# Order of mask tests, cell totals and scatter runs in a graph network kernel

## The reference

```python
edge_index = jnp.stack([src, dst])
h = jnp.maximum(_layernorm(x, axis=-1), 0.0)
x = x + _L0_gnn_ref(h, edge_index, ...)   # messages relu(bn([h[src], edge_rep[dst]] @ W1)), summed over dst, then over src
h = jnp.maximum(_layernorm(x, axis=-1), 0.0)
x = x + _L1_gnn_ref(h, edge_index, edge_weight, ...)   # three rounds of: sum over edges of norm * out[row]
...                                        # layer 2: attention over the first 3125 edges; layer 3: gated sum over edges
```

## Time and profile before

| what | us |
|---|---|
| median of 3 runs | 3788.69 (3786.29 to 3794.76) |
| the profiled execution | 3754.2 |
| its span | 3752.5 |
| TensorE busy | 2420.2 |
| VectorE busy | 2253.4 |
| ScalarE busy | 1348.1 |
| GpSimd busy | 1744.7 |

### The profile page before, as it was taken

One profiled execution on the slowest core, in us unless ns is written; L12 is line 12 of the kernel. 1 busy time (PEld: TensorE's weight loads), 2 busy tenths in 40 slices (PEclk: granted clock), 3 DMA queues, 4 the chain that ended last, 5 costly groups with the idle time before them and its releaser, 6 DMA issues. The chain is left out here.

```text
span 3752.5 us, 38369 instructions
## 1 busy us (share of the span) xinstructions
PE 2420.2 (64%) x11894; PEld 1975.0 (53%) x11894; DVE 2253.4 (60%) x4208; ACT 1348.1 (36%) x2765; POOL 1744.7 (46%) x1293
## 2 busy tenths in 40 slices
PE   5787544444444357750004998607999999973998
PEld 4422244444444345540004884406889888962688
DVE  6899677777777788860003442403564564535788
ACT  4488444434444200000002333303434434433676
POOL 0258877667667676767776767770000000024000
PEclk8888755555555568885557999758999999975999
DMA  9992355656556766651115661116546545512255
GB/s 350 355 322 26 49 169 170 169 168 173 167 164 172 161 158 184 187 124 0 0 0 122 177 156 1 1 0 171 171 132 187 173 132 171 162 53 53 84 174 177
DMA packets 339434, 521.99 MB, mean 139 GB/s; under 512 B 144970, under 2 KB 226691, under 8 KB 332195
## 3 DMA queue, kind: packets, MB, share of 16 engines
q1 hardware_dynamic: 197144, 446.27, 36.8%
q0 software_dynamic: 135920, 61.61, 14.2%
q10 hardware_dynamic: 6170, 11.66, 1.0%
HBM read 370.82 MB, written 148.58 MB: 138 GB/s over the span
## 5 line engine op out<-in xcount | busy, mean ns | idle before, releaser
L1054 PE MATMUL banks<-rows_r,lhs_r 128*128 128x448 f32 x3500 | 897.9, 371 | 517.4 <-issue 358.3
L1054 PEld LDWEIGHTS banks<-rows_r,lhs_r 128*128 128x128 f32 x3500 | 664.7, 190 | 588.6 <-issue 507.5
L669 POOL DMA_INDIRECT counts<-wts x391 | 615.2, 1573 | 378.2 <-issue 202.7
L678 POOL DMA_INDIRECT weights<-wts x391 | 634.0, 1621 | 253.5 <-issue 247.6
L498 DVE SCALAR_TENSOR_TENSOR ring_r<-ring,dinv,rows_r 128x896 fp32r<-128x896 f32 (+1 forms) x300 | 303.3, 1033 | 440.7 <-ACT rows_r L486 440.6
L686 POOL DMA_INDIRECT reg<-tab_p,w x440 | 426.1, 968 | 230.2 <-issue 120.5
L1054 PE MATMUL banks<-ring_r,lhs_r 128*128 128x448 f32 x1750 | 525.1, 370 | 0.0
L486 ACT ACTIVATE rows_r<-ring,dinv 128x896 fp32r<-128x896 f32 (+1 forms) x300 | 284.9, 951 | 515.0 <-PE banks L1054 345.1
L496 DVE TENSOR_TENSOR ring_r<-ring,rows_r 128x896 fp32r<-128x896 f32 x200 | 191.9, 973 | 445.1 <-ACT rows_r L484 444.8
L732 POOL DMA_INDIRECT el<-tab_l,base_i x25 | 24.0, 959 | 810.3 <-DMA tab_l<-reg 803.0
L484 ACT ACTIVATE rows_r<-ring 128x896 fp32r<-128x896 f32 x200 | 170.6, 857 | 510.2 <-DMA ring<-counts 358.9
(11 more groups left out here) (250 smaller groups left out, 3842.2 us busy)
## 6 DMA issues: line engine op xcount, KB each, us to landing
ring<-weights SPq DMA_DIRECT2D x225, 448.0 KB, 3.3
ring<-counts SPq DMA_DIRECT2D x150, 448.0 KB, 3.3
zbuf<-reg SPq DMA_DIRECT2D x220, 256.0 KB, 3.0
reg<-zbuf SPq DMA_DIRECT2D x55, 1024.0 KB, 4.7
counts<-ring SPq DMA_DIRECT2D x25, 1568.0 KB, 15.8
weights<-ring SPq DMA_DIRECT2D x25, 1568.0 KB, 17.6
ring<-cells SPq DMA_DIRECT2D x38, 448.0 KB, 4.3
ring<-weights SPq DMA_DIRECT2D x75, 224.0 KB, 3.2
```

The lines of the kernel that those rows point to most:

```text
L669: pool.indirect_dma_start(counts, bass.IndirectOffsetOnAxis(ap=ix_c[:, k:k + 1], axis=0), vals_c[:, k:k + 1], None, compute_op=ALU.add).th ...
L678: pool.indirect_dma_start(weights, bass.IndirectOffsetOnAxis(ap=ix_w[:, k:k + 1], axis=0), vals_w[:, k:k + 1], None, compute_op=ALU.add).t ...
L1054: m = pe.matmul(bank[:, 0:BLK], lhs[part], rows[:, c:c + BLK], start=first, stop=last)
```

## The change

Three things are altered, with no change in what is computed.

1. At a batch's end VectorE does `group_cells(g - 1)` first and `equal_cells(g)` after it.
2. TensorE no longer does `group_totals` at the end of its batch but in the next one, after the second pair and its degree columns (`q % 4 == 1`). The totals of the last group follow the last batch.
3. After the gathers (208 counts and 32 weights are issued by then) GpSimd issues 2 counts and 3 weights, which brings both to a border of groups, and then 26 times 7 counts and 4, 3 or 7 weights in turn, instead of 27 times 7 counts and 5 weights. The rest of the weights follows alone, as before.

```diff
--- before.py
+++ after.py
@@ -81,7 +81,7 @@
 assert SORT_G + len(P1_G) == GRP
 C_FIRST = 98
 C_PER = 1
-W_FROM, W_PER, W_MID = 42, 4, 5
+W_FROM, W_PER, W_MID = 42, 4, (4, 3, 7)
 
 class Signal:
 
@@ -713,9 +713,11 @@
                 gather(k)
                 if k % 4 == 3:
                     add_counts(C_PER)
-            while done_c < NE:
+            add_counts(-done_c % NG)
+            add_weights(-done_w % NG)
+            for k in range(-(-(NE - done_c) // NG)):
                 add_counts(NG)
-                add_weights(W_MID)
+                add_weights(W_MID[k % 3])
             add_weights(NE)
 
 
@@ -1153,8 +1155,10 @@
                     if i and i <= NBAT:
                         degrees(2 * q - 8)
                         degrees(2 * q - 7)
-                if i in P1_G:
-                    group_totals(SORT_G + P1_G.index(i))
+                    if q % 4 == 1 and i - 1 in P1_G:
+                        group_totals(SORT_G + P1_G.index(i - 1))
+            if NPASS - 1 in P1_G:
+                group_totals(GRP - 1)
             pe.wait_ge(z_acc, KQ + 1)
             for part in range(2):
                 for k in range(2):
@@ -1508,9 +1512,9 @@
                         sum_z(q - 1)
                 if i in P1_G:
                     g = SORT_G + P1_G.index(i)
-                    equal_cells(g)
                     if g > SORT_G:
                         group_cells(g - 1)
+                    equal_cells(g)
             sum_z(KQ - 1)
             v.wait_ge(z_acc, KQ)
             v.tensor_copy(zsum, zacc).then_inc(z_acc, 1)
```

## The result

The changed kernel takes **3702.55 us** (median of 4 runs, 3701.29 to 3704.19), the kernel before beside it 3791.73 us (4 runs, 3786.29 to 3800.76): ratio 0.9763, 95% interval 0.9742 to 0.9784. It is faster by 89 us, where 197 were predicted: the forecast of 3591 us (range 3572 to 3650) was too fast by 112 us. The profiled execution took 3703.68 us around its span of 3701.9.

The account below looks back on a forecast made before the run. GpSimd's queue up to the last weight scatter was taken as the bound; -98 (stalls) -105 (aligned runs) +6 (tail) = -197 us from the median of 3788.69 gave 3591 us, range 3572 to 3650.

Parts of the forecast that it names:

- I therefore take the whole stall but 2 us: -98 us.: Gather stage: of 100 us that GpSimd's gathers stall for VectorE's add_z, all but 2 go, -98 us.
- batches stay coupled, 3689: Rival, gather stage: TensorE's mid-batch wait or ScalarE's degree columns hold add_z as before, 98 us stay, 3689 us; chance 0.09.
- Waits that were to go: Group batches of the gather stage: VectorE's 130.5 us of waiting for TensorE falls to a few us.
- a step of 8.8 us: Group batch: the gap between VectorE's add_z around the tests falls from 12.02 to 8.8 us.
- 13.96 us a batch: Gather stage: the time GpSimd needs per batch without stalls, 768.0 us over 55 batches.
- Runs aligned with groups: Mixed counts and weights behind the gathers: all 41 drains at group borders are hidden, -105 us of 106.
- The estimate of 70 us: Mixed stretch: worth of 41 drains by the skill's fixed 2.0 us per transfer; the prediction kept 106 us instead.
- The tail: +6: Weights alone at the end: 34 drains rather than 32, at 2.8 us each, +6 us.
- 0.63 us each: Tail: worst-case extra for each of 13 moved weights while the first product runs, 8 us in all; nothing was charged.
- Points in time: End of the scatters: the last count starts near 1781 us, the last weight near 2342 us.

Follow-up runs that it names:

- e3: Kernel before with only the totals moved into the next batch and group_cells put first, runs as before: 3662.69 us, ratio 0.9748.
- e16: Changed kernel with each tile number loaded by TensorE two steps ahead, one per step: 3569.22 us, ratio 0.9497 to the kernel before.
- e5: Changed kernel, unaltered, on the second chip: 3715.17 us, ratio 0.9755 to the kernel before.
- e8: Changed kernel, unaltered, on the third chip: 3709.37 us, ratio 0.9733 to the kernel before.
- e12: Changed kernel, unaltered, on the fourth chip: 3711.32 us, ratio 0.9770 to the kernel before.
- e11: Kernel before, unaltered, profiled again on the third chip: 3804.08 us, ratio 0.9998.
- e1: Kernel before, unaltered, profiled again on the first chip: 3761.31 us, ratio 0.9996.
- e2: Kernel before with only the runs of counts and weights aligned with groups, on the first chip: 3663.84 us, ratio 0.9745.
- e10: Kernel before with only the runs of counts and weights aligned with groups, on the third chip: 3709.61 us, ratio 0.9749.
- e13: Changed kernel computing one of 28 products for each group of the passes, 2,106 TensorE instructions fewer: 3668.70 us, ratio 0.9649 to the kernel before.
- e7: Changed kernel with the totals of the passes' groups computed twice, 2,128 TensorE instructions more: 3729.32 us, ratio 0.9799 to the kernel before.
- e14: Changed kernel with a group's 28 products spread over the second to fourth step of the batch: 3767.50 us, ratio 0.9916 to the kernel before.
- e15: Changed kernel with one more DMA of 2,048 4-byte elements per batch on SyncE's queue: 3868.20 us, ratio 1.0173 to the kernel before.

## Why the prediction was wrong

**The failed step: "I therefore take the whole stall but 2 us: -98 us."** The mechanism was read rightly, and on chips of the first kind its size too: 868.6 to 776.5 us in e3, to 775.2 in e16. The result is of the second kind: the changed kernel's trace has the 900 us stage, the pauses of e5, e8 and e12 and 30,149 semaphore records, and the kernel before took 3791.73 us beside it, near the three chips of the second kind (3798.59 to 3810.28) and not the two of the first (3761.08, 3759.03). On such chips the stage takes 900 us before *and* after (e11, e8), so the term is 0. Without it the prediction's sum is -105 + 6 = -99 us; measured were -89 (result), -91 (e5), -101 (e8) and -87 (e12).

What I passed over was on the page. The profile that carries the argument took 3754.2 us, 34.5 under the median of the timed runs (it has 44,486 semaphore records: the first kind), and I added the 34.5 as if they lay outside the argument. They lay inside: e1's profile of this kernel and e11's differ by 40.0 us of span, of which 31.4 us are the gather stage and 18.5 us lie behind the last weight (1214.2 against 1232.7), with -12.7 us in the mixed stretch and the rest in small terms. The base was right at 3789 and the term was read from an execution of the other kind. The rival "batches stay coupled, 3689" had the right stretch and nearly the right price (14 us from the result) with a chance of 0.09, for a reason that is not this one.

**Waits that were to go.** On the first kind they went: VectorE waits 1.9 us for TensorE in place of 130.5. No gather of e3 idles more than 0.01 us beyond the gap of 0.30. So my model of how late VectorE may be was right there (a step of 8.8 us was predicted behind a group's tests, and 8.63 is the median of e3), and 13.96 us a batch is GpSimd's rate: e3's 776.5 / 55 = 14.1.

**Runs aligned with groups: right.** -105 of 106 was the term. Real stalls in the mixed stretch fell from 112 to 3 us on one chip (e1, e2) and from 99 to 4 on another (e11, e10), and the shorter stretch holds 11 weights fewer, which come later. The estimate of 70 us worked out from the fixed 2.0 us of the Trainium skill ("DMA: Bandwidth & Descriptors", anatomy of one DMA) was too little, as the rows of before said: a drain behind mixed runs idles 1.8 to 5.8 us beyond the gap in e1. The full cover by as few as three weights held: no gap at the head of a group is over 0.01 us beyond the 0.30 in e2, at 43 heads; in the changed kernel and in e16 one of the 43 idles 2.4 and 2.7 us, the first behind the gathers.

**The tail: +6 was right in kind and too large.** Its drains are 34 in place of 32, at 2.4 us beyond the gap, and all its stalls grew by 2 us: 79.0 + 9.6 to 81.7 + 8.7, drains and others. The 2.8 us a drain of the prediction had counted the others in. The rest of the stretch's +20.7 us is the 11 weights moved behind it, which the sum had counted in the mixed stretch. That they might pay 0.63 us each did not show in the mean, which is 1633 ns against 1644 before. By the Trainium skill, "SBUF — State Buffer", "Who interferes with whom", GpSimd's instructions can be blocked by VectorE's; no run here separates that.

**Points in time.** On the first kind the last count was to start at 1781 us and the last weight at 2342; in e16 they start at 1791.0 and 2350.1. With the result they are 1918.70 and 2473.77.

**What stays open.** Not settled is what causes the pause. Shown is that it belongs to the chip or to the conditions under which it was used: all traces of one chip are of one kind, on five chips (two of the first, three of the second), with the same instructions, the same granted clock and nearly the same busy times of all engines. It comes about every 33 us in e5, e7, e8 and e12, whether TensorE runs 2,128 instructions more or not, and less often with 2,106 fewer (some 20 delays in e13, 38 to 39 us apart). It is not a slower matmul or transfer: in the gather stage a product of `add_q` takes 451 ns in e1 and 453 in e11, and a packet of GpSimd's queue 116.2 and 116.6 ns. In the traces of the second kind semaphore records are missing, and in a pause those of all engines: between 844.18 and 852.03 us the result's trace has none but of DMA landings, though VectorE ended `add_z` at 845.24 and TensorE went on behind it. So taking the records may be what holds TensorE's reports back; nothing here shows how long the kernel takes without them, and that cause is only argued.

A rival to "pauses add up" is untested as well. On chips of the second kind the gather stage takes 896.7 to 901.8 us in all four kernels with the full totals once per group (before, runs only, totals only, changed), whether a wait is there to hide a pause or not. The pauses as I count them reach that number by two different sums, which may be luck, or a limit that all four share. e13's 39 us less and e7's 18 us more fit such a limit in sign, for it would grow with the instructions; e14's 58 us more at the same instructions do not. Not tried, since the last chip was of the first kind: whether a third bank hides it. The timeline around 852 us speaks against it, since the z computed ahead was reported late together with the one that was waited for.

## What to carry to other kernels

When the profiled execution lies outside the spread of the timed runs (here 34.5 us under a spread of 8), the difference is a stretch in which the two executions differ, and it is to be found before a gain is read from any one stretch; a second profile of the unchanged kernel shows it. A wait that an engine spends for another reason can cover delays that the profile doesn't show at all: the gain of removing it is bounded by what stands behind it, on every chip that the kernel is to run on. And a wait of a queue for its own transfers was the safer gain here, where other independent work could be put between: alone it was worth 2.5% on a chip of either kind.

## What the runs showed of the hardware

- The same program on different chips: 3759 to 3761 us on two, 3799 to 3810 us on three, medians of 7 to 19 runs of the kernel before on each.
- On the slower three, TensorE's increments of semaphores are held back about every 33 us, in the case shown by up to 9.4 us (the totals' end at 842.59, their report at 852.03), and come in bunches of up to seven within 0.4 us, at an unchanged granted clock of 0.50. This is seen in a stage with many short products (128x50, 128x4). What lies behind the last weight, with long products, is 9 to 19 us longer there, kernel for kernel (1213.4 and 1222.5 in e2 and e10, 1214.2 and 1232.7 in e1 and e11).
- A scatter of GpSimd that must wait for those of its own kind idles 1.8 to 5.8 us beyond the gap when mixed with others (e1), 1.8 to 6.7 us in the tail (e5), and nothing behind three or more others of another kind (5.85 us or more) at 43 of 43 heads in e2, at 42 of 43 in e16.
- 2,048 elements of 4 bytes more in a batch fill the 16 DMA engines: 0.97 busy at 138 GB/s (e15), where they were 0.58 busy at 161 GB/s in the changed kernel and 0.69 at 187 GB/s in e16.
